# Graph layer with an adjacency product in split precision: the three products of a chunk put together, with two of them on the same weights

## What is computed

```python
h = item_feat @ W_item.T + b_item            # 10000 x 128
b = x @ W_user.T + b_user                    # 10000 x 128
x = layernorm(x + relu(adj @ h + b))         # adj is 10000 x 10000, float32
```

## Time and profile before

| | |
|---|---|
| median of 3 runs | 1090.81 us |
| lowest and highest | 1089.79 and 1092.45 us |
| the profiled execution's own time | 1093.97 us |
| its span, first to last instruction | 1092.2 us |
| granted TensorE clock, mean | 0.998 |
| read from HBM and written to it | 411.67 MB and 5.18 MB |

### The profile page before, as it was taken

The page is one execution under the profiler, slowest core; times in us unless marked ns, Lnnn a source line. Parts: engine busy times, 40 slices in busy tenths (PEclk is TensorE's granted clock), DMA queues, the critical chain, the costliest instruction groups (busy, mean ns, idle before and its releaser), DMA issues.

```text
span 1092.2 us, 14905 instructions
## 1 busy us (share of the span) xinstructions
PE 1083.2 (99%) x4937; PEld 901.4 (83%) x4937; DVE 960.5 (88%) x619; ACT 842.9 (77%) x831; POOL 113.9 (10%) x56
## 2 busy tenths in 40 slices
PE   9999999999999999999999999999999999999997
PEld 9888888888888888888888888888888878888886
DVE  6998898989898989898989898989898989898986
ACT  6778787878787878787878787777777777878775
POOL 4360000000000000000000000000000000000000
PEclk9999999999999999999999999999999999999999
DMA  9999999999999999999999999999999999999985
GB/s 371 412 381 412 350 422 351 421 363 423 361 423 365 423 350 422 355 422 368 422 364 422 362 422 354 422 363 421 360 421 352 397 372 420 359 414 365 417 282 172
DMA packets 74741, 417.16 MB, mean 382 GB/s; under 512 B 8608, under 2 KB 19024, under 8 KB 28256
## 3 DMA queue, kind: packets, MB, share of 16 engines
q1 hardware_dynamic: 74576, 416.75, 96.9%
q10 hardware_dynamic: 144, 0.13, 0.0%
HBM read 411.67 MB, written 5.18 MB: 382 GB/s over the span
## 4 chain that ended last, share of the span: by engine, by line
PE 44%; issue 19%; ACT 15%; DVE 12%; DMA 9%; DVEq 1%; ACTq 0%; SPq 0%
PE acc L382 14%; PE acc L376 14%; PE acc L377 14%; ACT adj_hi L438 12%; DMA adj<-adj_t 7%; DVE adj_lo L633 7%; ACT gathered L469 1%; PE h_ps L360 1%; DMA adj<-adj_narrow 1%; DMA adj<-item_t 1%; DVE adj_lo L628 1%; DVE part L664 1%; DVE items L646 1%; DVE tail_pack L626 1%; DVE items L653 1%
## 5 line engine op out<-in xcount | busy, mean ns | idle before, releaser
L633 DVE TENSOR_TENSOR adj_lo<-adj,adj_hi 128x2048 fp32r<-128x2048 f32 (+2 forms) x399 | 864.9, 2184 | 115.9 <-ACT adj_hi L438 113.4
L438 ACT CAST adj_hi<-adj 128x2048 fp32r<-128x2048 f32 (+2 forms) x399 | 721.2, 1829 | 120.1 <-DMA adj<-adj_t 107.7
L376 PE MATMUL acc<-adj_hi,h_hi 128*128 128x512 f32 (+1 forms) x1580 | 605.3, 384 | 0.8 <-ACT adj_hi L438 0.7
L377 PE MATMUL acc<-adj_hi,h_lo 128*128 128x512 f32 (+1 forms) x1580 | 604.6, 384 | 0.0
L382 PE MATMUL acc<-adj_lo,h_hi 128*128 128x512 f32 (+1 forms) x1580 | 420.1, 385 | 0.6 <-DVE adj_lo L633 0.2
L376 PEld LDWEIGHTS acc<-adj_hi,h_hi 128*128 128x128 f32 x1580 | 296.7, 188 | 60.6 <-ACT adj_hi L438 1.8
L377 PEld LDWEIGHTS acc<-adj_hi,h_lo 128*128 128x128 f32 x1580 | 296.7, 188 | 58.5
L382 PEld LDWEIGHTS acc<-adj_lo,h_hi 128*128 128x128 f32 x1580 | 292.4, 188 | 62.0 <-DVE adj_lo L633 3.9
L585 POOL TENSOR_TENSOR items<-items,minus_mean 128x512 f32<-128x512 f32 x19 | 37.4, 1967 | 595.5 <-ACT minus_mean L477 595.5
L589 POOL TENSOR_TENSOR items<-items,rstd_all 128x512 f32<-128x512 f32 x19 | 37.6, 1981 | 337.8 <-ACT rstd_all L498 337.8
L469 ACT COPY gathered<-part 32x16 f32<-32x16 f32 x152 | 30.8, 203 | 38.5 <-DVE part L659 19.4
(11 more groups left out here) (49 smaller groups left out, 165.8 us busy)
## 6 DMA issues: line engine op xcount, KB each, us to landing
adj<-adj_t SPq DMA_DIRECT2D x360, 1024.0 KB, 7.8
adj<-adj_t SPq DMA_DIRECT2D x21, 512.0 KB, 5.2
adj<-adj_narrow SPq DMA_DIRECT2D x19, 544.0 KB, 5.4
xg<-x_t SPq DMA_DIRECT2D x19, 256.0 KB, 5.6
out<-items SPq DMA_DIRECT2D x19, 256.0 KB, 2.3
adj<-item_t SPq DMA_DIRECT2D x2, 1024.0 KB, 9.3
tail_in<-adj_tail SPq DMA_DIRECT2D x57, 32.0 KB, 4.5
items<-item_t SPq DMA_DIRECT2D x4, 256.0 KB, 4.4
```

Source lines behind the costliest of these rows:

```text
L376: nc.tensor.matmul(into, h_hi[:, k, :], adj_hi[:, s, c, 0:u], start=(k == 0), stop=False)
L377: nc.tensor.matmul(into, h_lo[:, k, :], adj_hi[:, s, c, 0:u], start=False, stop=False)
L438: nc.scalar.copy(adj_hi[:, s, start:, 0:u], adj[:, a, start:, 0:u]).then_inc(hi_made, 1)
L633: nc.vector.tensor_tensor(adj_lo[:, s, start:, 0:u], adj[:, a, start:, 0:u], adj_hi[:, s, start:, 0:u].bitcast(F32), ALU.subtract).then_in ...
```

## The change

In `tile_product` the three products of a chunk are issued one after the other, and both waits, for the high and for the low part, stand before the first of them. The order within a chunk becomes: `h_lo` with the high part, `h_hi` with the high part, `h_hi` with the low part, so that the second and the third have the same weights. The product that clears the bank (`start`) is now the first one with `h_lo`. The packed product is issued before the products of its part. Nothing else is changed.

```diff
                 for places, steps in parts(g, t):
                     pe.wait_ge(hi_made, steps)
-                    for c in places:
-                        k = chunk(t, c)
-                        nc.tensor.matmul(into, h_hi[:, k, :], adj_hi[:, s, c, 0:u], start=(k == 0), stop=False)
-                        nc.tensor.matmul(into, h_lo[:, k, :], adj_hi[:, s, c, 0:u], start=False, stop=False)
                     pe.wait_ge(lo_made, steps)
                     if t == LAST and AT_USER in places:
                         nc.tensor.matmul(into, h_pack[:, :], tail_pack[:, 0:u], start=False, stop=False)
                     for c in places:
-                        mm = nc.tensor.matmul(into, h_hi[:, chunk(t, c), :], adj_lo[:, s, c, 0:u],
-                                              start=False, stop=(t == LAST and c == PER_TILE - 1))
+                        k = chunk(t, c)
+                        last = t == LAST and c == PER_TILE - 1
+                        nc.tensor.matmul(into, h_lo[:, k, :], adj_hi[:, s, c, 0:u], start=(k == 0), stop=False)
+                        nc.tensor.matmul(into, h_hi[:, k, :], adj_hi[:, s, c, 0:u], start=False, stop=False)
+                        mm = nc.tensor.matmul(into, h_hi[:, k, :], adj_lo[:, s, c, 0:u], start=False, stop=last)
                 mm.then_inc(tile_done, 1)
```

## The result

| | before | after |
|---|---|---|
| median | 1092.45 us (15 runs) | 1094.83 us (15 runs) |
| lowest to highest | 1089.79 to 1094.02 | 1092.88 to 1099.69 |
| profiled execution, own time / span | 1093.97 / 1092.2 us | 1092.88 / 1091.0 us |

The ratio is 1.0025, with a 95% interval of 1.0016 to 1.0035: 2.7 us slower, within 1.7 to 3.8. That lies under the 0.3% that the forecast named as its limit of no change, but it is a real loss, and about four times the forecast one (1091.5 against a median of 1090.8 then, so +0.7 us). One execution of the kernel before, at 1859.49 us with a mean granted clock of 0.595, is left out of every comparison. The profiled execution of after happens to be 1.1 us faster than that of before; with runs that scatter over 4 us the two traces can't be subtracted, and have to be read for where the time goes.

What follows compares the result with a forecast made beforehand. TensorE was taken to pace the middle, with the feed an equal second bound, slower at the end. Terms 0 + 0 + 0.7 + 0 gave 1094.7 us profiled, 1091.5 us against the median 1090.81; range 1088.8 to 1095.5.

Steps and rivals of the forecast that it cites:

- step "sum": Whole kernel: 0 + 0 + 0.7 + 0, giving 1091.5 us against the median; within 0.3% at chance 0.80.
- a second bound: Loads and part-making on SP, ScalarE and VectorE: equal to TensorE within 0.1% in the middle, slower at the end.
- step 2: Same weights twice in each chunk: between 0 and 16.4 us of TensorE's time saved, taken as 0.
- A: TensorE is the bound and the pair is cheaper: 1075.1 us if the feed has hidden slack; chance 0.07.
- C: Pair cheaper, but the feed sets the end: 0.07 us less, 1091.4 us; chance 0.20.
- D: The order does nothing for the weights, each product loading its own at the same interval: 1091.5 us; chance 0.60.
- The first binding place: Tile 1 of group 0: the moved wait binds first there, TensorE beginning it at 28.46, near 28.5 us.
- the count at the end: Behind the last low part in the last group: six products left instead of two.
- rival B: ScalarE's wait for tile t-4: the lag fills the ring, up to 0.55 us per group, 1101.4 us at most; chance 0.13.
- step 4: Last group: the feed sets it and TensorE catches up, so the lag is not added; the end costs +0.72 us.
- step 3: Low-part wait moved to a tile's first product: TensorE 1.69 us behind from tile 1 of group 0.
- Step 5: Ring of four, tile 14 of group 11: ScalarE waits 0.55 us, absorbed, so 0; upper bound 9.9 us.

Runs made afterwards that it cites:

- experiment 5: The kernel before without the product of the low weights and the high part, a third of TensorE's work: 1091.81 us, ratio 0.9993.
- Experiment 4: The kernel before with the new order in the narrow last group alone: 1094.11 us, ratio 1.0013.
- Experiment 10: The new order everywhere except in tile 1 of group 0 and in the last group, against the kernel before: 1091.48 us, ratio 1.0000.
- experiments 2: Against the kernel before: four h_lo products under the high part's wait, then the low part's wait, then four pairs with equal weights: 1091.83 us, ratio 0.9995.
- Experiment 3: The kernel before with the new order in tile 1 of group 0 alone, the old one in 399 tiles: 1093.85 us, ratio 1.0014.
- 9: The new order everywhere except in tile 1 of group 0, against the kernel before: 1093.48 us, ratio 1.0016.

## Why the prediction was right, and what it sized wrongly

**Right, and shown.** The time changes by less than 0.3% (step "sum"). The feed is a second bound equal to TensorE: experiment 5, with a period of 53.85 us. Equal weights in a row bring nothing (step 2, taken at 0): 1580 loads and 226.7 ns in the changed kernel, and again with three equal sets. Of the rivals, A and C are out by these two; D, the forecast, holds for the weights. The first binding place, about 28.5 us, was right too, and so was the count at the end: two products need the last low part before, six after.

**Luck in the number.** The measured median, 1094.83 us, is 3.3 us above the forecast and 0.7 us under the top of the range, and it lies beyond the 1094.1 that the prediction had named for "slower by over 0.3%". It is within 0.3% because the median of before, 1090.81 in the three runs that the forecast stood on, is 1092.45 in fifteen. The range reached up to 1095.5 for the sake of rival B, whose price was not found. The direction was forecast; the size, +0.7 us, is about a quarter of the +2.7 (1.7 to 3.8) that the runs show.

**Sized wrongly: step 4, the end.** It gave +0.72 us for the stretch behind the last low part and its predecessor; the traces give 1.30 - 0.40 = 0.90. My sum let tile 18 begin 0.06 us after its low part and ran every product of it at 0.125 us, so that TensorE was done with it at the moment when the last low part was ready. In the changed kernel the low part of tile 18 is ready at 1079.59 + 1.29 = 1080.88, the tile begins at 1081.03, 0.15 us later, and its first product takes 0.20 us. So when the last low part is ready at 1082.43, TensorE is still at tile 18 and has eleven products to start (its last one, and ten). Experiment 4 confirms the term by its trace (1.30 us), and its time agrees (+1.4, 0.1 to 2.7).

**Missing: the clock, in step 3.** I counted the idling of tile 1 as a lag of 1.69 us and nothing more. The lag itself is 2.0 us in the changed kernel's trace (from the start of the last product of tile 0 to that of the first of tile 2 it has 5.14 us, the kernel before 3.15). Behind some 2 us of idling the granted clock can fall to the lower level for a tile, which adds 1.7 us to the lag in a quarter to a half of the executions, and 1.5 us (0.9 to 2.2) to the time of these. For the changed kernel's 15 runs that is 7/15 x 1.5 = 0.7 us on average. The Trainium skill has a case of it: "TensorE: Matmul & The Clock Gate", on oscillation in real kernels, describes a TensorE that waits for its next tile, falls back to half clock and runs the tile cold; the waits there are of 3 to 5 us. The trace agrees in kind, 0.43 us per product, and here 1.82 to 2.10 us of idling were enough. Nothing of it stood in the forecast: I looked at the clock of the kernel before, which is busy in that place.

**Step 5, the ring: one place in the sum, 16 groups in the trace.** The premise holds: in the kernel before the ring is nowhere full, and its tightest wide place is the one named, with 1.14 us. There the changed kernel waits 0.80 us, where the forecast said 0.55. But the sum looked at this one place, and a right forecast was to show itself by waits of ScalarE for TensorE of under 1 us each; they come in 40 places, and the longest is 1.6 us, so that sign failed. Rival B's mechanism is there, many of the waits at the tiles that it named (13, 14 and the next group's 1), and its price is not: it wanted a period over 54.5 us, and the period is 54.01. Experiment 10 has waits for the ring in six groups and loses nothing.

**Half right: step 4's claim that the last group takes the lag up.** It fits lags up to 1.25 us (experiments 2 and 10: no loss). For the whole lag it is not shown. Experiment 3 without its executions at 0.997 or less averages 1093.3 us, where the executions of before beside it average 1092.4: 0.9 more, but with an interval of -0.2 to +1.9, and some of these may hold the slow tile too. Its trace speaks against a lag that is carried whole. Its last group begins at 1051.54, where that of the kernel before begins at 1050.60 and that of experiment 10, which loses nothing, at 1051.88:

```profile
1051.54 0.28 PE L387 MATMUL acc<-adj_hi,h_hi 128*128 128x272 f32 x1
...
1051.88 0.28 PE L387 MATMUL acc<-adj_hi,h_hi 128*128 128x272 f32 x1
```

By then some of the lag has gone into the time that the kernel before loses to late low parts in groups 15 to 18. The ring is full in three places of experiment 3, all in the first three groups, for 1.5 us. Whether that is how a lag of 2 us costs something stays open: one profile for each kernel can't tell, and no run here widens the ring.

Taken together for the changed kernel: 0.9 us at the end (shown in the traces), 0.7 us by the clock (an estimate from the clocks of the runs, and a lower bound of their share), and about 1 us that is left of the 2.7, with an uncertainty as large as itself. The lag is the candidate for it; its cause is not shown.

**What the busy share would have told.** By the 99% of its products TensorE was the engine to relieve. "Perfetto Trace Analysis" of the Trainium skill, on the most-contended engine, says that the busy share of matmuls "is not a good measure of how close you are to roofline", and takes FLOPs and the busy share of the weight loads in its place. The weight loads stand at 83%, under VectorE's 88%. The trace agrees so far that the 99% decided nothing: relieving TensorE of a third of its work changed nothing (experiment 5). Moving one store two tiles later, which takes work from no engine, gained 1.4 (0.3 to 2.4) and 1.6 us (0.4 to 2.7).

## What to carry to other kernels

An engine at 99% busy is not alone the bound when the chain that feeds it has the same period: measure the feed's own period from a mark that comes once per round, and try it with less work on the busy engine before trading anything for that engine's sake. Moving a wait ahead of work that covered it costs little in the steady state, where the data are ahead, and shows at the two ends: at the start, where the first data are late, and behind the last piece, where all that was covered is now exposed. Where only part of the cover is needed, give up only part: with four products under the first wait the loss is too small to measure, with none it is 2.2 us. And before counting a wait that the profile names, look whether the producer that it names had long been done: eight of ScalarE's waits in the kernel before were put down to TensorE and were not for it.

## What the hardware showed that I had not expected

- One idle stretch of about 2 us on TensorE lowered its granted clock to 0.58 over the 4.1 us around the next tile in some executions and not in others: behind 1.82, 2.08 and 2.10 us of idling it fell in three profiles, behind 1.95 and 2.20 us it stayed at 1.00 in two. The stretches of 1.02, 1.39 and 1.08 us in experiments 2, 9 and 10 are not followed by slow products.
- Three products in a row on the same weights load these weights three times, and neither the load (188 ns) nor the interval (226.7 ns for 512 columns) becomes shorter. At 512 columns the load is shorter than the interval.
- Less reading by TensorE did not speed up the transfers here: with a third of the products gone the DMA engines moved the same 422 GB/s in the full stretches and some 360 in the others.
